# All pair blocks first, all single blocks last, in the expert stage of a two-layer kernel

## The chip, the cores and the metric

The kernel runs on one core of a Trainium2 chip. The metric is the device time in microseconds of one execution. Before the change three runs took 1934.67, 1937.21 and 1942.63 us; the median is 1937.21 us.

The engines are TensorE (PE), VectorE (DVE), ScalarE (ACT), GpSimd (POOL) and SyncE (SP). SP computes nothing here: it issues DMA transfers, in program order, and waits on semaphores between them. POOL issues the transfers that go by an index table.

## The reference, cut to what matters

The whole computation is two layers, each of an attention and a feed-forward part. The change touches only the last part, a mixture of experts over 1600 tokens of width 512, with seven routed experts of which each token takes two, and one shared expert that every token takes:

```python
gate = (xt @ Wr + br) / TEMP
_, ids = jax.lax.top_k(gate + gate_bias, TOPK)         # TOPK = 2 of 7 experts
probs = softmax over the two chosen logits
u = jnp.einsum('nh,ehi->eni', xt, Wup) + bup[:, None, :]
g = jax.nn.silu(jnp.einsum('eni,eij->enj', u, Wgate) + bgate[:, None, :]) * u
eo = jnp.einsum('enj,ejh->enh', g, Wdown) + bdown[:, None, :]
out = jnp.einsum('ne,enh->nh', probs, eo) + shared expert of the same form
```

All matrices are 512 x 512 in fp32, so one expert has three matrices (up, gate, down) of 1 MiB each.

## The kernel before, in words

The kernel works through four stages one after the other; the expert stage (`expert_ffn`) is the last. It runs through 26 **blocks** of tokens, numbered j = 0 to 25. A tile is 128 tokens. Blocks 0 to 5 are the shared expert on two tiles each, block 6 is the shared expert on its thirteenth and last tile. Blocks 7 to 25 are the routed ones: 12 **pairs** (two tiles of one expert) and 7 **singles** (one tile). Which expert a block belongs to is found at run time by the router, whose result lies in a table of slots; how many pairs and singles there are, and at which block number each stands, is fixed in the list `ROUTED` (line 1967), from which `is_pair(j)`, `place_of(j)`, `table_tile(j, i)`, `version_of(j)` and the other small functions follow. In the list of before, a pair and a single alternate as long as there are singles, and five pairs are left over: pairs at blocks 7, 9, 11, 13, 15, 17, 19 and 21 to 25, singles at blocks 8, 10, ..., 20.

A pair and a single are computed in different ways. A pair splits each fp32 operand into a high and a low part in a rounded format and multiplies three times (high x high, low x high, high x low). Its weights land in `ex_raw_weights`, ACT copies them into `ex_weights_high` (line 2264), and DVE subtracts to get `ex_weights_low` (line 2380). The raw buffer of a matrix is free for the next pair as soon as the low part is made. A single multiplies plain fp32 from `raw_s`, a second set of three buffers in memory that held the activations before (the profile calls it `residual`). A buffer of `raw_s` is free only when PE has done the matmuls that read it. There is one such buffer for each matrix.

PE's order (at the end of `expert_ffn`): `gate(j)`, `up(j+1)`, `down(j)`, `turn(j+2)` for each j, where `turn` transposes the gathered rows of a block. Up of a pair is line 2823, up of a single 2819; gate is 2854 and 2848; down is 2877 and 2871; turn is 2797.

SP's order (from line 2229): for j = 7 to 25, it reads the expert of the block and issues three loads, up, gate, down. Ahead of each load of a pair it waits until the low part of the previous pair's matrix is made. Ahead of each load of a single it waits until PE has finished with that matrix in the single before (`single_before(j)`): the up matmuls, the gate matmuls, or all down matmuls.

POOL gathers the rows of block j+3 during block j, makes the low half of a pair's product `g` (line 2766), and adds the finished tiles of the block before into `out` by indirect transfers (line 2735). ACT makes the high parts, the silu and the first output tile, DVE the low parts, the product and the second output tile. A pair's u is kept in `uh` and `ul`, and DVE reads u for the product from PSUM; a single's u lies in `us`, of which there is one buffer, and DVE reads it there.

Of the kernel before, what the change touches and what calls it, by code (L numbers as in the profile page):

```python
# [24 lines left out]
KC = D // 128  # L25
# [1923 lines left out]
NP = (RT - E) // 2  # L1949
NS = RT - 2 * NP  # L1950
# [7 lines left out]

def routed_order():

    order = []
    for k in range(max(NP, NS)):
        order += [("pair", k)] * (k < NP) + [("single", k)] * (k < NS)
    return order


ROUTED = routed_order()


def is_pair(j):  # L1970
    return j < SH_TILES // 2 or (j >= SH and ROUTED[j - SH][0] == "pair")
# [40 lines left out]
def version_of(j):  # L2012

    return 0 if j < SH else pairs_before(j) - pairs_before(SH) + 1
# [17 lines left out]
def expert_ffn(core, w_exp, b_exp, b_down, w_router, b_router, order, tokens, out):  # L2032
# [5 lines left out]
    with ExitStack() as own:  # L2038
# [3 lines left out]
        def sem(name):  # L2042
            return core.sem(tag + name)
# [68 lines left out]
        g_psum, g_silu, g_mul, g_high, g_low = sem("g_psum"), sem("g_silu"), sem("g_mul"), sem("g_high"), sem("g_low")  # L2112
# [4 lines left out]
        def width(j):  # L2117
            return BT * tiles_of(j)

        def new_weights(j):  # L2120
            return SH <= j < BLOCKS and is_pair(j)

        def upb(j, c, n):
            return ps[:, 6 * (j % 2) + c % 2, c // 2 * BN:c // 2 * BN + n]
# [10 lines left out]
        def bias_of(j, m, c):  # L2135
            v = place_of(j) + 1 if j >= SH else 0
            return bsel[:, v, m * KC + c:m * KC + c + 1]
# [37 lines left out]
        with nc.Block() as block:  # L2175
# [77 lines left out]
            def _(act):  # L2253
                def high(v, m):
                    act.wait_ge(w_in[m], (v + 1) * 16)
                    if v:
                        i = pair_before(first_block(v))
                        if m == UP:
                            act.wait_ge(u_psum, (i + 1) * KC)
                        elif m == GATE:  # L2260
                            act.wait_ge(g_psum, (i + 1) * KC)
                        else:
                            act.wait_ge(d_psum, first_tile(i + 1))
                    act.copy(wh[:, m, :], raw[:, m, :]).then_inc(w_high[m], 1)  # L2264
# [27 lines left out]
                def up_high(j):  # L2292
                    n = width(j)
                    act.wait_ge(bias_ready, 1 if j < SH else 2)
                    for c in range(KC):
                        act.wait_ge(u_psum, j * KC + c + 1)
                        dst = uh if is_pair(j) else us
                        act.activation(dst[:, c, :], upb(j, c, n), ACT.Identity, bias=bias_of(j, UP, c)).then_inc(u_high, 1)
                        if c == 1 and new_weights(j):
                            high(version_of(j), GATE)  # L2300
# [38 lines left out]
                block_high(0)  # L2339
                high(0, GATE)  # L2340
                up_high(0)
                high(0, DOWN)
                act.wait_ge(d_exp, 1)
                act.activation(hit[:], hit[:], ACT.Exp).then_inc(r_exp, 1)
                block_high(1)
                for j in range(BLOCKS):
                    gate(j)
                    if j == 0:
                        turn_probs(0)
                    if j + 1 < BLOCKS:  # L2350
                        up_high(j + 1)
                    if j == 0:
                        turn_probs(1)
                    if new_weights(j + 2):
                        high(version_of(j + 2), UP)
                    if j == SH:
                        act.wait_ge(tab_in, 16)
                    first_out(j)
                    if new_weights(j + 1):
                        high(version_of(j + 1), DOWN)  # L2360
                    if j + 2 < BLOCKS:
                        block_high(j + 2)
# [707 lines left out]
```

## Time and profile before

| what | value |
|---|---|
| median of 3 runs | 1937.21 us (1934.67 to 1942.63) |
| profiled execution | 1938.36 us, of which the span of instructions is 1936.2 us |
| granted TensorE clock, mean | 0.981 of full speed |
| routed blocks 7 to 25 with the drain | about 1631 us to the end of the span |

The profiled execution is one run under the hardware profiler. "Busy" counts time in which an engine executes, without its waits. A time in the rows is counted from the span's start. Matmuls overlap, so the difference between two starts says more than one duration. PEclk is the TensorE clock granted, in parts of full speed (2.4 GHz); 0.50 is 1.2 GHz.

### The profile page before, as it was taken

How to read it: one execution, taken by the hardware profiler on the slowest of the kernel's cores; microseconds unless marked ns; L12 is line 12 of the kernel's file. 1: busy time of each engine (PE TensorE's matmuls, PEld its weight loads, DVE VectorE, ACT ScalarE, POOL GpSimd, SP SyncE). 2: the span in 40 equal slices, each digit the busy share in tenths (PEclk: the TensorE clock that was granted, in tenths of full speed). 3: DMA queues.
4: the chain of work that ended last, by engine and by line, in shares of the span. 5: the costliest groups of instructions: out<-in, count | busy, mean ns of one | idle time of the engine just before them, and what ended most of it. 6: DMA issues, size and time to landing. Idle time of an engine off the chain costs nothing. (4 is left out here: it accounts for less than half of the span.)

```text
span 1936.2 us, 30897 instructions
## 1 busy us (share of the span) xinstructions
PE 1788.7 (92%) x11108; PEld 1427.5 (74%) x11122; DVE 1318.7 (68%) x2912; ACT 913.4 (47%) x2005; POOL 600.3 (31%) x582
## 2 busy tenths in 40 slices
PE   8899999999899999999997999899987989999997
PEld 7677887778777887778775544666665878888896
DVE  6777677776687778887777896477676633444564
ACT  3544445433543445434543654555544324555563
POOL 5333122331633122321211131232231454343353
PEclk9999999999999999999998999899999989999999
DMA  5022211210121222222204111000005267787773
GB/s 213 17 89 86 65 42 69 89 61 33 67 79 37 95 80 67 76 97 81 81 17 206 36 40 39 25 1 1 1 22 171 59 190 224 241 282 265 238 236 77
DMA packets 49672, 188.52 MB, mean 97 GB/s; under 512 B 7388, under 2 KB 11612, under 8 KB 38260
## 3 DMA queue, kind: packets, MB, share of 16 engines
q1 hardware_dynamic: 39396, 166.86, 23.9%
q0 software_dynamic: 9840, 19.70, 5.3%
q8 instruction: 91, 1.49, 0.3%
q14 instruction: 57, 0.47, 0.1%
q10 hardware_dynamic: 288, 0.00, 0.0%
HBM read 158.29 MB, written 28.24 MB: 96 GB/s over the span
## 5 line engine op out<-in xcount | busy, mean ns | idle before, releaser
L442 POOL TENSOR_TENSOR la_q_roped<-la_q_roped 128x400 f32<-128x400 f32 x128 | 134.7, 1074 | 657.2 <-DVE la_q_roped L976 657.2
L869 ACT ACTIVATE la_probs<-banks,la_minus_max 100x361 f32<-100x361 f32 x256 | 144.8, 566 | 179.5 <-DVE la_minus_max L1087 179.5
L976 DVE TENSOR_TENSOR la_q_roped<-banks,la_rope_q 128x400 f32<-128x400 f32 x384 | 198.0, 567 | 34.9 <-PE banks L557 26.1
L611 PEld LDWEIGHTS banks<-identity,la_probs 100*121 100x121 f32 x768 | 111.2, 184 | 78.6 <-DVE la_probs L1094 54.1
L1094 DVE TENSOR_SCALAR la_probs<-la_probs,la_rsum 100x361 f32<-100x361 f32 x256 | 154.8, 605 | 9.1
L650 PE MATMUL banks<-la_ctx_parts,la_wout_high 128*128 128x416 f32 (+3 forms) x512 | 158.6, 361 | 2.0 <-DVE residual L1028 1.7
L611 PE MATMUL banks<-identity,la_probs 100*121 100x100 f32 x768 | 127.5, 274 | 31.2 <-DVE la_probs L1094 18.8
L1087 DVE TENSOR_REDUCE la_minus_max<-banks 100x1 f32<-100x361 f32 x256 | 134.8, 527 | 28.0 <-PE banks L602 26.0
L2380 DVE TENSOR_TENSOR ex_weights_low<-ex_raw_weights,ex_weights_high 128x2048 fp32r<-128x2048 f32 x39 | 89.4, 2292 | 93.5 <-ACT ex_weights_high L2264 93.5
L622 PE MATMUL banks<-la_probs_t,la_kv_rows 121*128 121x200 f32 x768 | 152.3, 334 | 0.0
L887 ACT COPY la_probs_t<-banks 121x300 f32<-121x300 f32 x256 | 104.8, 409 | 60.3 <-PE banks L611 60.0
L622 PEld LDWEIGHTS banks<-la_probs_t,la_kv_rows 121*128 121x128 f32 x768 | 132.0, 190 | 0.3
L797 ACT CAST la_q_high<-banks 128x400 fp32r<-128x400 f32 x64 | 31.6, 495 | 179.5 <-PE banks L539 179.5
L1107 DVE TENSOR_TENSOR la_ctx_parts<-banks,la_ctx_parts 128x200 fp32r<-128x200 f32 (+2 forms) x144 | 48.0, 342 | 94.8 <-ACT la_ctx_parts L879 94.5
L602 PE MATMUL banks<-la_kv_t_high,la_qk_high 128*100 128x362 f32 x256 | 101.6, 397 | 2.9 <-ACT la_probs L869 2.7
L1300 PE MATMUL banks<-qf_sign_weights,qf_x_quant_t 128*128 128x512 bf16 (+1 forms) x403 | 95.8, 390 | 6.4 <-DVE qf_hidden L1435 2.9
L574 PE MATMUL banks<-la_q_roped,la_weights 128*64 128x400 f32 x512 | 96.6, 508 | 4.9 <-POOL la_q_roped L442 4.9
L650 PEld LDWEIGHTS banks<-la_ctx_parts,la_wout_high 128*128 128x128 f32 x512 | 95.5, 189 | 6.3 <-DVE residual L1028 3.3
L2766 POOL TENSOR_TENSOR ex_g_low<-ex_g,ex_g_high 128x256 fp32r<-128x256 f32 x72 | 56.7, 831 | 134.0 <-ACT ex_g_high L2312 133.8
L539 PE MATMUL banks<-la_xn_t_high,la_wq_high 128*128 128x400 f32 x256 | 95.9, 375 | 0.8 <-DVE la_xn_t_low L951 0.8
L2735 POOL DMA_INDIRECT out<-ex_block_out,ex_slots x31 | 57.0, 1840 | 118.8 <-ACT ex_block_out L2324 110.0
L1659 POOL TENSOR_TENSOR ca_probs<-ca_probs,ca_rsums 100x400 f32<-100x400 f32 x64 | 54.7, 855 | 123.2 <-DVE ca_rsums L1882 122.9
(380 smaller groups left out, 5055.1 us busy)
## 6 DMA issues: line engine op xcount, KB each, us to landing
ex_raw_weights<-w_exp SPq DMA_DIRECT2D x39, 1024.0 KB
la_weights<-w_pack SPq DMA_DIRECT2D x15, 1856.0 KB, 7.7
residual<-w_exp SPq DMA_DIRECT2D x24, 1024.0 KB, 7.5
la_kv_turned<-w_ffn SPq DMA_DIRECT2D x30, 384.0 KB
la_rope_k<-w_ffn SPq DMA_DIRECT2D x30, 384.0 KB, 3.4
qf_sign_weights<-ffn_signs SPq DMA_DIRECT2D x3, 2048.0 KB, 7.9
ffn_signs<-la_ffn_signs SPq DMA_DIRECT2D x30, 192.0 KB, 2.0
out<-ex_block_out POOLq DMA_DIRECT2D x13, 256.0 KB
```

The lines of the kernel that those rows point to most:

```text
L442: pool.tensor_tensor(roped[:, h, 0, c, :], roped[:, h, 0, c, :], roped[:, h, 1, 1 - c, :], ALU.add).then_inc(b_add, 1)
L539: mm = pe.matmul(ps[:, unit_bank(n, u), 0:NT], a[:, k, wc], b[:, k, xs], start=(k == 0 and j == 0), stop=(k == KC - 1 and j == 2))
L574: mm = pe.matmul(ps[h * R:(h + 1) * R, C_BANKS[run], 0:NT], w["r"][:, j, h, :], roped[:, h, v, c, :], start=(j == 0), stop=(j == len(STEPS ...
L602: mm = pe.matmul(ps[0:S, j % 2, 0:LE], a[:, h, qs], c[:, b, :], start=(k == 0), stop=(k == 2))
L611: mm = pe.transpose(ps[0:LC, T_BANK, c * S:(c + 1) * S], prob[:, j % 4, c * LC:(c + 1) * LC], core.ident[0:S, 0:S])
L622: mm = pe.matmul(ps[:, V_BANK, 0:2 * S], kv[:, b, c, :], probt[:, b % 2, c, :, :].rearrange("p h s -> p (h s)"), start=(c == 0), stop=(c = ...
L650: mm = pe.matmul(ps[:, out_bank(n, run, k), 0:count], a[:, h, kc], c[:, h, :], start=(h == 0 and j == 0), stop=(h == 1 and j == 2))
L869: act.activation(prob[:, s % 4, 0:L], ps[0:S, s % 2, 0:L], ACT.Exp, bias=nmax[:, s % 4:s % 4 + 1], accum_out=sums[:, s % 4:s % 4 + 1]).the ...
L887: act.copy(probt[:, b % 2, :, j % 2, :], ps[0:LC, T_BANK, 0:LCN * S].rearrange("p (c s) -> p c s", c=LCN)).then_inc(t_out, 1)
L976: dve.tensor_tensor(roped[:, h, v, c, :].rearrange("p (b s) -> p b s", b=GB), ps[:, B_BANKS[k % 2], 0:NT].rearrange("p (b s) -> p b s", b=GB),
L1087: dve.tensor_reduce(nmax[:, s % 4:s % 4 + 1], ps[0:S, s % 2, 0:L], AX.X, ALU.max, negate=True).then_inc(s_max, 1)
L1094: dve.tensor_scalar(prob[:, j % 4, 0:L], prob[:, j % 4, 0:L], rsum[:, j % 4:j % 4 + 1], None, ALU.mult).then_inc(s_norm, 1)
```

## The change

The list of routed blocks is put in another order: the 12 pairs stand first, at blocks 7 to 18, and the 7 singles last, at blocks 19 to 25. Every engine's program is generated from this list, so loads, gathers, copies, matmuls and scatters all move with it; their number stays the same. Since singles now follow each other, and `us` is a single buffer, ACT gets a wait in `up_high`: before it writes u of a single that follows a single, all products of the block before must be done.

```diff
 def routed_order():
-    order = []
-    for k in range(max(NP, NS)):
-        order += [("pair", k)] * (k < NP) + [("single", k)] * (k < NS)
-    return order
+    return [("pair", k) for k in range(NP)] + [("single", k) for k in range(NS)]
...
                 def up_high(j):
                     n = width(j)
                     act.wait_ge(bias_ready, 1 if j < SH else 2)
+                    if not is_pair(j) and not is_pair(j - 1):
+                        act.wait_ge(g_mul, j * KC)
                     for c in range(KC):
                         act.wait_ge(u_psum, j * KC + c + 1)
```

Here NP = 12, NS = 7, SH = 7 (the number of shared blocks) and KC = 4 (chunks of 128 in a width of 512).

## Rows read from the trace of the kernel before

**Rows 1.** The head of the page: busy time of each engine.

```profile
PE 1788.7 (92%) x11108; PEld 1427.5 (74%) x11122; DVE 1318.7 (68%) x2912; ACT 913.4 (47%) x2005; POOL 600.3 (31%) x582
```

**Rows 2.** Windows: length, busy PE, PEld, DVE, ACT, POOL, clock, DMA share, GB/s.

```profile
1779.69:1809.45 29.76, 29.37 (x205) 25.98 (x205) 13.35 (x17) 15.90 (x28) 11.08 (x10) 1.00 0.80 265
1839.26:1857.38 18.12, 18.12 (x128) 16.89 (x129) 12.54 (x14) 12.11 (x18) 8.64 (x8) 1.00 0.77 258
1857.38:1875.23 17.85, 17.85 (x131) 16.84 (x130) 12.26 (x14) 11.82 (x18) 11.01 (x9) 1.00 0.73 223
```

**Rows 3.** Waits of PE, 1600 to 1905: total us, times, longest.

```profile
PE banks L2854 <- issue: 2.7, 7, 0.4
```

**Rows 4.** Chain of waits, around a single, then a pair round: start, us.

```profile
1808.62 0.44 PE banks L2797 x4
1809.06 0.39 issue
...
1815.44 1.78 PE banks L2819 x16
...
1819.28 5.48 PE banks L2877 x24
...
1825.63 3.57 PE banks L2848 x32
...
1834.95 3.43 PE banks L2871 x8
...
1857.62 5.76 PE banks L2854 x48
1863.38 5.75 PE banks L2823 x48
1869.13 5.47 PE banks L2877 x24
```

**Rows 5.** Timeline of DVE, the low part of turned rows: start, us.

```profile
1860.99 1.22 DVE L2389 TENSOR_TENSOR ex_block_t_low<-banks,ex_block_t_high 128x1024 fp32r<-128x1024 f32 x1
```

**Rows 6.** Timeline of SP's queue: a single's down load, then two of a pair.

```profile
1808.79 0.33 SPq L2245 DMA_DIRECT2D residual<-w_exp  x1
1809.88 0.85 SPq L2245 DMA_DIRECT2D ex_raw_weights<-w_exp  x2
```

**Rows 7.** Timeline: two loads issued together, and ACT's wait for the second.

```profile
1843.71 1.47 SPq L2245 DMA_DIRECT2D ex_raw_weights<-w_exp  x2
...
1852.51 1.92 ACT L2264 CAST ex_weights_high<-ex_raw_weights 128x2048 fp32r<-128x2048 f32 x1 [0.72 <-DMA ex_raw_weights<-w_exp]
...
1879.09 1.43 SPq L2245 DMA_DIRECT2D ex_raw_weights<-w_exp  x2
...
1888.31 1.91 ACT L2264 CAST ex_weights_high<-ex_raw_weights 128x2048 fp32r<-128x2048 f32 x1 [0.81 <-DMA ex_raw_weights<-w_exp]
```

**Rows 8.** Landing after issue: routed loads (line 2245); three together (2227).

```profile
DMA to landing us min/median/max: 5.3/7.6/8.2
...
DMA to landing us min/median/max: 7.0/7.0/7.0
```

**Rows 9.** Windows at two gaps of PE, and PE's timeline at the second.

```profile
1550.50:1554.50 4.00, 0.00 (x0) 0.00 (x0) 0.75 (x1) 0.00 (x0) 0.00 (x0) 0.75 0.54 149
1554.50:1559.30 4.80, 4.78 (x23) 4.78 (x24) 1.23 (x1) 1.23 (x2) 0.00 (x0) 0.50 0.97 386
1594.60:1600.20 5.60, 5.54 (x13) 4.37 (x14) 0.00 (x0) 0.69 (x1) 2.06 (x3) 0.50 0.28 47
...
1594.66 0.79 PE L2877 MATMUL banks<-ex_weights_high,ex_g_high 128*128 128x512 f32 x1 [3.38 <-POOL ex_g_low L2766]
```

**Rows 10.** Timeline of DVE: last product of a single.

```profile
1829.64 0.29 DVE L2413 TENSOR_TENSOR residual<-residual,ex_silu_gate 128x128 f32<-128x128 f32 x1 [0.60 <-issue]
```

**Rows 11.** Timeline of POOL: the scatter of a single, and the last scatter.

```profile
1809.62 1.62 POOL L2735 DMA_INDIRECT out<-ex_block_out,ex_slots  x1 [9.38 <-ACT ex_block_out L2324]
...
1925.06 1.55 POOL L2735 DMA_INDIRECT out<-ex_block_out,ex_slots  x1 [1.01 <-DVE ex_block_out L2432]
```

## The prediction

> **What bounds the kernel now.** I read the engine totals first: TensorE (PE) is busy for 92% of the span, no other engine over 68% [rows 1]. The change touches only the routed blocks of the last stage, so all else is read there. The windows show what one round of the present order (one pair block and one single block) costs: 29.76 us with PE busy for 29.37 of it, and one round of the pair blocks that already stand together at the end: 17.85 us with PE busy for all of it, the first of two alike [rows 2]. Over the routed stretch PE waits 2.7 us in all, 0.4 us at a time, and for no load [rows 3]. So this stretch is bound by matmuls, and the order of blocks can gain little on PE: the arithmetic is the same. The question is what the loads do when the blocks that PE finishes fastest, each with 3 MiB of weights, stand together.
>
> The chain of waits gives the phases (differences of starts) [rows 4]. Pair: gate 5.76, up 5.75, down 5.47, and the rest of the 17.85 us for turn, 0.87. Single: up 3.84 (1815.44 to 1819.28), gate 3.57, down 3.43, turn 0.44 and 0.39 until the turned-out bank is free (0.83 together), in all 11.67 us. PE's order is gate(j), up(j+1), down(j), turn(j+2).
>
> **The pair run (blocks 7 to 18).** What is moved: 12 pair blocks stand together, with their 36 weight loads on SP's queue, 24 gathers and 24 scatter-adds on POOL's, and the high and low copies of weights on ACT and DVE. The last blocks of the old order are just that, and there the weight copies, gathers and scatters all fit in 17.85 us with no idle PE: ACT is busy 11.8 us of it, DVE 12.3, POOL 11.0 [rows 2]. The smallest cover I see is the low half of the next block's turned rows: DVE ends it at 1862.2 (1860.99+1.22) and PE's up starts at 1863.38 [rows 4, 5], about 1.2 us of slack. I cost the run at 17.85 per block, nothing extra; if the cover were gone, it would be some 1 us for each of ten blocks. The entry (single 6, pair 7, pair 8) is the same sequence as single 20, pair 21, pair 22 of before, whose first round took 18.12 [rows 2].
>
> **The single run (blocks 19 to 25).** The singles work from one raw buffer per matrix, each refilled only after its last use, and SP issues in program order: UP(j), GATE(j), DOWN(j), then UP(j+1). DOWN(j) has to wait until down(j-1) is over. Call that moment T. UP(j+1) stands behind it on SP, though up(j) was over 3.4 us earlier. In the old order that does no harm: the next thing behind a single's DOWN is a pair's load into another buffer, and the next single is a whole pair block away: down ended at 1808.62, DOWN was issued at 1808.79, and the load behind it at 1809.88 [rows 4, 6]. In the new order that load is UP(j+1), and PE wants it after turn (0.83) and gate(j) (3.57), at T+4.4.
>
> When does it arrive? Issue is at T+0.17 and T+1.26 by these rows. Three times before, SP issued two 1 MiB loads 1.1 us apart and ACT then waited for the second; in the first and the last of them the issue is at 1843.71 and 1879.09, ACT's copy starts at 1852.51 and 1888.31 [rows 7]. That is 8.80 and 9.22 us after the first issue, with POOL's gather of two tiles going on beside it. In the single run one scatter and one gather fall on the same place, so I take 9.0, between the two: UP(j+1) is there at T+9.2, and PE idles **4.8 us**. From both sides: a lone 1 MiB load landed in 5.3 us at best and 8.2 at worst [rows 8]; three issued at once landed 7.0 after their issue, nothing beside them [rows 8]. The second can't be earlier than about 7.4 after the first issue by that (stall 3.2), and with the worst lone row plus the 1.1 us and some more contention it is 10.3 (stall 6.1).
>
> The Trainium skill, page "DMA: Bandwidth & Descriptors", section "Anatomy of one DMA — SWDGE (gpsimd) path", fits a transfer as about 2.0 us fixed plus its bytes over 436 GB/s; for 2 MiB that makes an estimate of 6.8 us instead of the 9.0 read above, a stall of 2.6. The rows with other traffic beside decide for me; the fit belongs with the second rival.
>
> How often? UP(19), GATE(19), DOWN(19) go into buffers idle since block 6 and are issued behind pair 18's loads, one pair block early: hidden. UP(20) waits only for up(19), since DOWN(19) was issued long before; PE wants it after down(18), turn and gate(19), 5.47+0.83+3.57 = 9.9 us later, against 5.3 to 8.2 for a lone load [rows 4, 8]: hidden. UP(21), 22, 23, 24, 25: stalled. **Five stalls.** GATE(j+1), issued when gate(j) ends, has over 13 us; DOWN(j), the first of the two, lands before up(j+1) ends. DOWN(25), behind T of the last round, lands some 5.3 us later, when the last gate's result is ready anyhow (0.83+3.57+about 1): nothing.
>
> **The clock.** PE's granted clock is full (2.4 GHz) in these rounds [rows 2]. Earlier in the same stage it fell twice: after 4.0 us without PE work (1550.5 to 1554.5) the next 4.8 us ran at 0.50 (1.2 GHz), and after a gap of 3.38 us (to 1594.66) the next 5.6 us did [rows 9]. Gaps of 4.8 us are longer than both. Half of 4.8 and of 5.6 us is 2.4 and 2.8 lost. The slow stretch ended 8.8 us after the first gap began (1550.5 to 1559.3) and 8.9 us after the second (1591.3 to 1600.2), so with PE back only after 4.8 us there would remain 4.0 to 4.1 us at half speed, 2.0 lost. I take **2.3 us** per stall; bounds 0 (no fall) and 3.3 (a slow stretch half as long again).
>
> The Trainium skill speaks against this change: "TensorE: Matmul & The Clock Gate", section "HAM oscillation — how this bites in real kernels", describes a loop in which each wait for a load drops the clock again, so that each next piece starts cold. This trace agrees in its two gaps; that it would happen five times in a row no row of it shows.
>
> **The added wait.** ACT's up_high of a single after a single waits for the last product of the block before, since both use one u buffer. Behind it on ACT are that block's silu, its output copy, and PE's third up chunk. The last product of a single's gate ended at 1829.93 (1829.64+0.29) [rows 10], 0.73 us after gate's end (1825.63+3.57), and the first up chunk isn't finished before 3.84/4 = 0.96 us after that end: nothing. In the single run up comes after a stall besides. Uncovered it is under 1 us for each of six, so up to 6 in all, and below nothing there is no gain in a wait.
>
> **What is saved.** The mixed round costs 29.76 against 17.85+11.67 = 29.52: 0.24 us for each of the six whole rounds, 1.4 us [rows 2, 4]. At the end, a single drains faster than a pair: the last pair's second tile goes out in a second scatter at 1925.06, waiting for DVE, with 1936.2 as the end, and its down needs a low half that POOL makes [rows 11]. A single has no low half and one scatter, which starts 1.0 us after its down (1808.62 to 1809.62) [rows 4, 11]. I take 1.1 us. Together **-2.5 us** (bounds 0 and -5).
>
> **Sum.** 5 x (4.8 + 2.3) = 35.5, less 2.5 = +33 us on the profiled execution's 1938.36 (span 1936.2 and 2.2 around it): 1971. That execution stands 1.2 above the median 1937.21 of the runs shown, so the forecast is **1970 us**. Its own range is 1962 to 1977.
>
> **Rivals.**
> A. The stalls come, the clock holds. For it: the two falls are single gaps, and rows of repeated ones don't exist here; against it: both are shorter than 4.8 us. 5 x 4.8 - 2.5 = +21.5: 1959. Chance 0.12.
> B. The loads land sooner, because in the single run far less goes over DMA in a round (3 MiB and two tiles in over 16 us, against 6 MiB and six tiles in 29.76). Then the stall is 3.2 and the clock falls sometimes: 5 x 3.2 to 5 x 4.2, less 2.5: +13 to +18, 1951 to 1956. Chance 0.12. The skill's DMA fit named above would give 5 x 2.6 - 2.5 = +10.5, 1948, the low end of this.
> C. More goes wrong in the same direction: landing at T+10.4 and a loss of 3.3, or the pair run's 1.2 us of cover is gone. 5 x 9.3 - 2.5 = +44, 1981, or 1970 + 10. Chance 0.13.
> D. Not slower: UP(j+1) is there when PE wants it, and only the 2.5 us are left, 1935. It is decided at SP's queue: the second load would have to land within 4.2 us of the first issue, where even a lone first one took 5.3. It would be so if SP had passed the wait on down(j-1) already, which the code excludes. For it speaks only that before no single's load was waited for. Chance 0.05.
> The forecast has 0.58.
>
> **Numbers.** About 0.5% (10 us) is what a measurement of this kernel can tell from no change. Slower by more: forecast, A, C and nearly all of B, 0.93. Within 0.5%: D and the low end of B, 0.06. Faster: 0.01. The range is 1951 to 1982: it takes in A, B from its row-based low end, and C.
>
> **What would show it.** Right: the timeline of PE's up phase of blocks 21 to 25 has five gaps before it of 4 to 6 us, ended by the DMA of the single buffer; the clock row has 0.50 right after each; SP issues DOWN(j) 0.2 us after down(j-1) ends and UP(j+1) 1.1 us later; pair rounds are 17.85 us with no gap and lie from about 1631 to 1843; single rounds are near 18.8 us instead of 11.7. The last round's down shows no such gap. Wrong: single rounds near 11.7 us (D), rounds near 16.5 us at full clock (A), gaps before gate or down as well, or pair rounds over 18 us (C). A gap before block 20's up would be a miscount of the stalls, some 7 us each.

## The result, and the profile after

The new kernel takes 1973.46 us (median of 4 runs, 1972.84 to 1974.51) against 1938.31 us of the old one beside it; the ratio is 1.0175, 95% interval 1.0160 to 1.0189. It is slower by 35 us. Forecast was 1970 us, 33 us more.

The head of the page after: PE is still busy for 92% of the span, but the last two of the 40 slices of the clock row, which were 9 before, are 8. The last row below is the clock row of the old kernel.

```profile
span 1970.5 us, 30911 instructions
PE 1804.3 (92%) x11122; PEld 1442.3 (73%) x11122; DVE 1319.2 (67%) x2912; ACT 914.0 (46%) x2005; POOL 613.2 (31%) x582
...
PEclk9999999999999999999999998999999999999988
...
PEclk9999999999999999999998999899999989999999
```

The windows of the new kernel, in the columns of [rows 2]: two rounds of pairs, then four rounds of singles, and last the first gap of PE in the single run.

```profile
1650.98:1668.83 17.85, 17.85 (x131) 16.84 (x130) 12.27 (x13) 11.82 (x18) 10.58 (x8) 1.00 0.76 228
1668.83:1686.68 17.85, 17.85 (x131) 16.84 (x130) 12.26 (x13) 11.81 (x18) 10.92 (x9) 1.00 0.80 237
...
1874.11:1891.80 17.69, 13.12 (x78) 10.79 (x77) 1.17 (x4) 4.11 (x10) 2.57 (x2) 0.90 0.60 207
1891.80:1911.60 19.80, 14.43 (x79) 12.10 (x77) 1.17 (x4) 4.10 (x10) 2.58 (x2) 0.83 0.53 187
1911.60:1929.29 17.69, 13.12 (x79) 10.79 (x77) 1.17 (x4) 4.10 (x10) 1.56 (x1) 0.90 0.56 193
1929.29:1949.28 19.99, 14.33 (x77) 11.69 (x74) 1.17 (x4) 4.10 (x10) 1.56 (x1) 0.83 0.50 171
...
1860.10:1863.90 3.80, 0.00 (x0) 0.00 (x0) 0.29 (x1) 0.37 (x1) 0.00 (x0) 0.91 1.02 303
```

The pair rounds are what they were in [rows 2], 17.85 us with no idle PE. A single round takes 17.7 to 20.0 us (18.8 on average) where its phases add up to 11.67 [rows 4]. Over a whole round the DMA engines are *less* busy than before (0.50 to 0.60, against 0.80 in a mixed round), though they are fully busy (1.02) within the first gap, when the loads have at last been issued. That speaks for a late issue and not for a lack of rate over the round; the experiments test it.

PE's waits from 1600 on, as in [rows 3], now have one large line. Line 2818 is the up of a single; the profile names no releaser ("issue").

```profile
PE banks L2818 <- issue: 22.5, 5, 5.3
PE banks L2847 <- issue: 2.4, 5, 0.8
PE banks L2847 <- DMA residual<-w_exp: 0.7, 1, 0.7
PE banks L2870 <- DMA residual<-w_exp: 0.7, 1, 0.7
```

The chain of waits shows where the five lie, in the form of [rows 4]: after gate (2847), before up (2818). Two of them:

```profile
1870.67 3.44 PE banks L2870 x8
1874.11 0.44 PE banks L2796 x4
1874.55 0.39 issue
1874.93 3.81 PE banks L2847 x32
1878.74 4.18 issue
1882.93 5.44 PE banks L2818 x32
1888.37 3.44 PE banks L2870 x8
...
1892.62 3.81 PE banks L2847 x32
1896.43 4.98 issue
1901.41 6.75 PE banks L2818 x32
```

The gaps are 3.89, 4.18, 4.98, 4.18 and 5.26 us, and up after them runs for 6.70, 5.44, 6.75, 5.44 and 6.64 us, where it takes 3.57 behind a single's gate without a gap. SP's queue at the first of the two, and the landing of the second load in it, as in [rows 6, 8]: down's load is issued 0.17 us after down(j-1) ended at 1874.11, up's 1.1 us later. Up's load lands 7.5 us after its own issue, at 1882.9, which is when up starts. For the five stalls that landing took 7.5, 7.5, 7.9, 7.5 and 8.5 us.

```profile
1874.28 1.43 SPq L2242 DMA_DIRECT2D residual<-w_exp  x2
...
DMA to landing us min/median/max: 7.5/7.5/7.5
```

To compare traces without what lies ahead of the changed part, I use the stretch from the start of block 6's gate to the end of the span: 319.0 us before (1617.17 to 1936.2), 351.7 after (1618.8 to 1970.5), **+32.7 us**. The remaining 1.6 us of the two spans' difference was there before block 6, in blocks that are the same; the executions of the old kernel alone differ by 8 us. Where I speak of "the stretch" below, it is this one, in the profiled execution of each run.

### The profile page after: what moved, and what is told of

Read it like the earlier page. It is cut to its first block and busy times, and to the rows that moved or that the text cites. A ratio compares the mean times of both kernels' runs of the same rounds, so it can differ in the third digit from the quotient of the medians.

```text
span 1970.5 us, 30911 instructions
## 1 busy us (share of the span) xinstructions
PE 1804.3 (92%) x11122; PEld 1442.3 (73%) x11122; DVE 1319.2 (67%) x2912; ACT 914.0 (46%) x2005; POOL 613.2 (31%) x582
## 5 line engine op out<-in xcount | busy, mean ns | idle before, releaser
L2765 POOL TENSOR_TENSOR ex_g_low<-ex_g,ex_g_high 128x256 fp32r<-128x256 f32 x72 | 60.8, 950 | 143.7 <-ACT ex_g_high L2311 143.4
```

## The experiments

The theory: up(j+1) stands in SP's program order behind a wait on down(j-1) that it doesn't need itself, lands late, and the gap makes the clock fall. Rivals were the rate of the DMA engines, the added wait on ACT, and slow reads in place of a slow clock. Each run is compared with runs of the old kernel on the same chip, whose median was between 1937.5 and 1940.4 us.

### Up's load ahead of down's

```diff
+                loads = [(j, m) for j in range(SH, BLOCKS) for m in range(MATS)]
+                for j in range(SH + NP + 1, BLOCKS - 1):
+                    at = loads.index((j, DOWN))
+                    loads[at:at + 2] = [(j + 1, UP), (j, DOWN)]
...
```

> New order of blocks; in the single run SP issues up(j+1) ahead of down(j), and nothing else is changed. Theory (queue order: the up load stands behind a wait on down(j-1) that it doesn't need): up(j+1) is issued 3.4 us earlier and lands near the end of gate(j); down(j) lands some 8 us after down(j-1), just when it is wanted. Gaps of 0 to 1 us, no fall of the clock, 1935 to 1942 us. Rival 1 (3 MiB per single round of 11.7 us are more than the DMA engines carry): the gaps move ahead of down or gate and stay about 4 us, 1958 to 1975. Rival 2 (the wait that the change adds on ACT): 1973, as after.

Measured: 1940.29 us, ratio 0.9992 (0.9978 to 1.0006); the stretch takes 316.3 us. One swap in the order of issue, in each of five rounds, gives the whole loss back. The same bytes move in rounds of 11.8 us, so the rate of the DMA engines was not the limit. The chain now goes through the gate loads, which just fail to be early (0.6 us at most): line 2854 (gate of a single) follows a load of 7.7 us.

```profile
1853.60 3.82 PE banks L2854 x32
...
1857.58 7.72 DMA residual<-w_exp
1865.30 0.08 issue
1865.37 3.82 PE banks L2854 x32
```

### Two sets of buffers

```diff
+                            i = single_before(j) if j == SH + NP else j - 2
+                            if j == SH + NP + 1:
+                                sp.wait_ge(w_low[m], NP + 1)
...
+                            dst, arrived = single_mats(j)[:, m, :], single_in(j, m)[0]
```

> New order of blocks; the singles of the last run use two sets of weight buffers in turn, their own and the one that the pairs have left free, so that each load waits for the block two before. SP's order is unchanged. Theory: no gap is left, 1934 to 1938 us, i.e. 35 us come back, and the 2.5 us that the order itself saves can be seen. Rival 1 (rate of the DMA engines): with buffers to spare the rate still holds, rounds above 13 us, over 1945. Rival 2 (wait on ACT): 1973.

Measured: 1937.02 us, ratio 0.9982 (0.9970 to 0.9994); stretch 315.3 us. SP's order is the old one, but its waits are on the block two before, so the load behind them is early. The profile shows no wait of PE that a load ended, and none over 0.8 us, and rounds take 11.64 us by the starts of down:

```profile
1864.58 3.44 PE banks L2883 x8
...
1868.84 3.81 PE banks L2860 x32
1872.65 3.57 PE banks L2831 x32
1876.22 3.44 PE banks L2883 x8
```

### Four singles last

```diff
-    return [("pair", k) for k in range(NP)] + [("single", k) for k in range(NS)]
+    mixed = [x for k in range(3) for x in (("pair", k), ("single", k))]
+    return mixed + [("pair", k) for k in range(3, NP)] + [("single", k) for k in range(3, NS)]
```

> Order of blocks: three rounds of pair and single, then nine pairs, then four singles. Theory (the first two singles of a run find their loads ready, each later one stalls): two stalls of 7 us, less 2: 1950 us, two gaps ahead of up in the trace. Rival (a run of singles stalls from its second block on, or the cost is that of the long pair run): 1957, or no change against the run of seven, 1973.

Measured: 1954.98 us, ratio 1.0071 (1.0050 to 1.0093), which is 5 us more than expected; stretch 330.2 us, 11.2 more than before, where 12 was expected. PE waits ahead of up twice, 4.28 and 5.67 us, and the up after each takes 5.18 and 5.92 us. In a last run of four two stall, in one of seven five: the count holds.

### The gap filled with matmuls

```diff
+                        if j >= SH + NP + 2:
+                            pe.wait_ge(g_mul, (j - 2) * KC + 3)
+                            for _ in range(18):
+                                pe.matmul(upb(j, 0, n), core.ident[:], core.ident[:], start=True, stop=True)
                         pe.wait_ge(s_in[UP], 16 * (singles_before(j) + 1))
```

> New order of blocks; PE runs 18 fp32 matmuls on the identity (0.22 us each, 4.0 us) ahead of the up of blocks 21 to 25, into the bank that up then overwrites. They fill the gap with work that nobody needs. Theory (gap plus a fall of the clock that follows from it): the gap stays as long as the load takes, but the clock stays at 1.00 and up runs in 3.57 us in place of 5.3 to 6.6: 12 us less, 1961 us. Rival (up is slow because its operands come late or DMA traffic slows the reads, not by the clock): up stays at 5.3 to 6.6 us, 1973.

Measured: 1965.49 us, ratio 1.0121 (1.0099 to 1.0142), some 10 us below the new kernel by the ratios; stretch 343.5. The windows over two rounds show the clock at 1.00 (so do those over the other three):

```profile
1858.00:1876.00 18.00, 15.88 (x115) 13.44 (x115) 1.17 (x4) 4.83 (x12) 2.64 (x3) 1.00 0.60 205
1876.00:1893.00 17.00, 15.60 (x114) 13.24 (x114) 1.17 (x4) 4.16 (x11) 2.62 (x3) 1.00 0.64 217
```

and the chain names what the profile of the new kernel called "issue": SP issues down's load (line 2242), then reads the expert (2228), then up's load runs, and PE's up (2822) starts as it lands and takes 3.84 us.

```profile
1871.51 3.45 PE banks L2874 x8
1875.11 0.33 SPq L2242
...
1875.49 0.27 SPq L2228
...
1876.20 8.36 DMA residual<-w_exp
1884.61 3.84 PE banks L2822 x32
```

The slow up was the clock. 1961 was too low: of the 12 us expected, 8.2 came on the stretch. Four of the five loads of up landed 8.4 to 8.9 us after their issue here, against 7.5 to 8.5 in the new kernel. From the end of down(j-1) to the start of up it was 48.9 us over the five rounds, against 46.0, so some 3 us went there. Why they landed later no run shows.

### A quarter of down's bytes

```diff
+                        if m == DOWN and j > SH + NP:
+                            sp.dma_start(dst[:, 0:D], w_exp[bass.ds(e, 1), m, :, 0:D].rearrange("e p d -> p (e d)")).then_inc(arrived, 16)
+                            continue
```

> New order of blocks; in blocks 20 to 25 the down load moves only the first 512 of 2048 columns of its matrix (256 KiB in place of 1 MiB), so the rest of the down weights is left out. The wait on down(j-1) and SP's order stay. Theory (up(j+1) is late by its place in the queue, and how late depends on the bytes ahead of it): up lands some 2.3 us sooner, five gaps of 2.0 to 2.5 us in place of 4.5; such gaps let the clock fall at most now and then; 1938 - 2.5 + 11 = 1947 us, up to 1955 if the clock falls each time. Rival (the landing is latency, whatever is ahead): gaps of 4.5 us, 1970.

Measured: 1950.65 us, ratio 1.0055 (1.0039 to 1.0070); stretch 335.1 us. Four gaps are 2.0 to 2.5 us, as the theory said, and one is 4.6, which it did not; 13.4 in all (the first, of 2.04, isn't in the rows below; up took 5.44 after it), against 22.5. So with 768 KiB less ahead of it up's load lands sooner, mostly by some 2 us; the other 7 us or so from the end of down(j-1) to its landing stay. Why one gap stayed long is open. What I hadn't expected is that the clock fell after three of the five gaps, short ones among them:

```profile
1873.69 2.22 issue
1875.90 3.81 PE banks L2821 x32
...
1887.79 4.62 issue
1892.40 5.42 PE banks L2821 x32
...
1905.89 2.05 issue
1907.94 3.81 PE banks L2821 x32
...
1919.82 2.51 issue
1922.33 5.44 PE banks L2821 x32
```

### Two buffers for u, without the added wait

```diff
-                    if not is_pair(j) and not is_pair(j - 1):
-                        act.wait_ge(g_mul, j * KC)
...
-                        dst = uh if is_pair(j) else us
+                        dst = uh if is_pair(j) else us_of(j)
```

> New order of blocks; the singles' u lies in two buffers in turn, so the added wait of ACT on the products of the block before is not needed and is gone. Weights and SP's order as in the new kernel. Theory (the wait is hidden): 1973 us, within 2 us of the new kernel, five gaps of 3.9 to 5.3 us as there. Rival (the wait holds ACT up, and through it PE's third chunk of up): rounds of singles get shorter by up to 1 us each, 1967.

Measured: 1976.65 us, ratio 1.0185 (1.0168 to 1.0201), which overlaps the new kernel's interval. The five gaps ahead of up are there as well, 4.2 to 6.0 us and 25.4 in all, somewhat more than the 22.5 of the new kernel. Taking the wait away gives nothing.

### Twos in turn

```diff
...
+    order = []
+    for k in range(0, NP, 2):
+        order += [("pair", k), ("pair", k + 1)] + [("single", i) for i in (k, k + 1) if i < NS]
+    return order
```

> Order of blocks: two pairs, two singles, in turn, and pairs for the rest (the last single alone). One set of buffers as in the new kernel. Theory (in a run of n singles only n-2 stall, since the first two find the buffers free long before): no stall at all, although singles follow each other; 0 to 2 us below before. Rival (a single behind a single stalls): three gaps, 1955 to 1960.

Measured: 1975.70 us, ratio 1.0178 (1.0163 to 1.0193); stretch 353.2 us. Both expectations were wrong: three gaps, but of 10 us each, and ahead of *gate* of the second single. The timelines of SP and ACT at one of the three show why. SP issues the second single's down load at 1749.1, when the first single's down is over, and only then, at 1750.19, the next pair's up load. ACT, in order, stands for 11.39 us at the high copy of that very matrix, and the output copy (2326) that frees PE's bank for the next gate is behind it:

```profile
1742.08 7.34 SPq L2245 DMA_DIRECT2D residual<-w_exp  x2
1750.19 1.37 SPq L2245 DMA_DIRECT2D ex_raw_weights<-w_exp  x3
...
1757.28 1.90 ACT L2264 CAST ex_weights_high<-ex_raw_weights 128x2048 fp32r<-128x2048 f32 x1 [11.39 <-DMA ex_raw_weights<-w_exp]
1759.08 0.68 ACT L2326 ACTIVATE ex_block_out<-banks,ex_slots 128x512 f32<-128x512 f32 x1
...
1749.79 10.07 issue
1759.86 6.05 PE banks L2850 x32
```

So the same wait on SP, with another load behind it, costs more. My rule (n-2 of a run stall) was borne out only for runs at the very end (four and seven singles), with no pair behind.

### Twos, with the pair's up load earlier

```diff
...
+                    if not is_pair(j - 1) and not is_pair(j) and is_pair(j + 1):
+                        loads.remove((j + 1, UP))
+                        loads.insert(loads.index((j, GATE)), (j + 1, UP))
...
```

> Order of blocks as in the run with twos (two pairs, two singles, in turn); SP issues the up load of the pair that follows two singles ahead of the second single's gate and down loads. Theory formed on the trace of the twos (the three gaps of 10 us come from that load standing on SP behind the wait on the first single's down, while ACT, in order, waits for it ahead of the output copy that frees PE's bank): the three gaps go, 35 us come back, 1936 to 1942 us. Rival (a single behind a single is slow in itself, by its own loads or banks): three gaps of 5 us or more stay, over 1955.

Measured: 1951.93 us, ratio 1.0072 (1.0053 to 1.0090); stretch 330.3 us. Neither number was hit. 23 of the 34 us come back on the stretch, and the gaps of 10 us are down to 0.8 or 0.9 us each ahead of the single's gate. Three smaller gaps (8.5 us in all) now stand a block later, ahead of the pair's gate, where ACT waits 3.58 us for a further weight load, at 1755.97, again with an output copy behind it. Behind two of these gaps (3.07 and 3.01 us) the clock falls and the pair's gate takes 7.46 and 7.48 us in place of 5.76; behind the third (2.43) it stays at 1.00 and the gate takes 6.17. The two rows are from ACT's timeline at the third:

```profile
1755.97 1.90 ACT L2272 CAST ex_weights_high<-ex_raw_weights 128x2048 fp32r<-128x2048 f32 x1 [3.58 <-DMA ex_raw_weights<-w_exp]
1757.77 0.68 ACT L2334 ACTIVATE ex_block_out<-banks,ex_slots 128x512 f32<-128x512 f32 x1
```

### Both pairs of buffers

The edit joins that of the two sets with that of the two u buffers.

> New order of blocks, with two sets of weight buffers for the last singles and two buffers for u, so that neither loads nor ACT's added wait can hold a single up. Theory: as with two sets alone, 3 us below before (0.1 to 0.2%), since ACT's wait costs nothing; the stretch from block 6's gate to the end takes 315 us in place of 319.0. Rival (ACT's wait costs something once the loads no longer hide it): 1 to 3 us less than with two sets alone, 313 us or less for that stretch.

Measured: 1936.40 us, ratio 0.9981 (0.9967 to 0.9994); stretch 315.2 us, against 315.3 with two sets alone. ACT's wait costs nothing here either. With 0.2% it is the best version beside that with two sets, and both are faster than the old kernel by about as much as can be told.

## Why the prediction was right

**The pair run** was costed at 17.85 us a block and nothing extra. It took that, and from block 6's gate to the single run PE shows no wait. (The rows bear out the block time; the cover of 1.2 us was not tested.)

**The place and the number of the stalls** were right: five, ahead of the up of blocks 21 to 25. The two experiments on SP (order, buffers) show the cause, since each leaves the bytes and the order of blocks alone and brings the time back.

**The stall** was put at 4.8 us (24.0 in all); measured 22.5, or 4.5 each. Up was to be there 9.2 us after down(j-1)'s end and was there after 8.9, 8.8, 9.6, 8.8 and 9.9, on average 9.2. The two waits of [rows 7], which had a gather of two tiles beside them, were good measures for it. What was too short is the other side: PE wanted up 4.6 us after that end and not 4.4, because the gate of a single behind the short wait for the bank takes 3.81 us and not 3.57, and in the first round 5.0, because that gate waited for its own load besides.

**The clock** was put at 2.3 us a stall (11.5). Up took 30.97 us in the five rounds in place of 5 x 3.57 = 17.85, so 13.1 us more; 0.27 of each is the start after any gap (3.84 with the clock at 1.00, in the run with the filled gap), which leaves 11.8. Rival A (the clock holds) is out. The sum is right, but in part by luck. The working had the slow stretch end about 8.8 us after the gap began; it ended 8.4 to 11.2 us after, and the loss was 1.6 us behind two gaps and 2.8 to 2.9 behind three. The 2.3 lies between the two kinds. The Trainium skill, page "TensorE: Matmul & The Clock Gate", section "HAM oscillation — how this bites in real kernels", describes a loop in which the wait for each load drops the clock again. The new kernel's trace agrees: it fell anew in each of five rounds.

**What is saved** was put at 2.5 us. The runs with the stalls removed show it alone: 316.3, 315.3 and 315.2 us against 319.0, so 2.7 to 3.8 less. Counted up from the 315.3 of the two sets, the gaps (22.5), the slower up (13.1) and 0.5 more for short waits make 351.4, against 351.7 measured. So the saving was nearer 3.7, a little more than forecast. How it divides between the rounds (1.4 by the forecast) and the end (1.1) no run shows.

**The added wait** was put at nothing: shown twice.

**Rival B** had the stall at 3.2 us, because far less goes over DMA in a single round. Less did go (a busy share of 0.50 to 0.60), but the second load landed no sooner for it, and the smallest gap was 3.89 us. The Trainium skill, page "DMA: Bandwidth & Descriptors", section "Anatomy of one DMA — SWDGE (gpsimd) path", has a fit by which the two loads would take an estimated 6.8 us. It is given for transfers that GpSimd issues, and these come from SP. The trace shows 8.6 us from the first issue at 1874.28 to 1882.9, and up to 9.6 in the other rounds.

**Missed, but small:** gate of block 20 waited 0.7 us for its load. The prediction gave every gate load over 13 us of cover, which counts a stall in between; ahead of block 20 there is none yet, and the cover is only the 7.4 us of up, down and turn, against a landing 8.1 us after the end of the gate before. Down of block 25 waited 0.7 us as well, where I had called it nothing and had counted a turn (0.83 us) that the last round doesn't have.

A weak point that luck hid: I counted stalls by asking only when each *single's* load is free to go. The twos showed that every load behind the waiting one has to be followed, through ACT too. In the new order there is no pair behind the run, so the count came out.

## What to carry to other kernels

SP's queue here issues loads in program order with waits between them, and so a load goes out no sooner than the last wait ahead of it ends, whether it needs that wait or not. Before blocks of a kind are put together, write down for each load which wait stands before it in the queue, when that wait ends, and when the load is wanted; if the wait belongs to a later use than the load's own, swap them or give the buffer a twin. Follow the load to the end, through the engines that wait for it in order. And add the clock: behind the five gaps of 3.9 to 5.3 us it cost another 1.6 to 2.9 us each. Behind the three gaps of 10 us in the run with twos it was no more: the gate took 5.45, 6.05 and 6.25 us in place of 3.84.

## What I had not expected of the hardware

The stretch at 0.50 was 3.4 or 6.8 us long in the clock's records of the new kernel, in turn with the gaps (3.89: 6.8; 4.18: 3.4; 4.98: 6.8; 4.18: 3.4; 5.26: 6.8), and up ran 5.4 or 6.7 us by it. The windows over two ups show it, in the columns of [rows 2]; the first of them began at full clock, which fell only 0.8 us after PE had resumed.

```profile
1882.93:1888.37 5.44, 5.44 (x33) 5.44 (x34) 0.00 (x0) 1.10 (x3) 0.00 (x0) 0.69 0.53 218
1901.41:1908.17 6.76, 6.75 (x33) 6.76 (x34) 0.00 (x0) 1.10 (x3) 0.00 (x0) 0.54 0.33 136
```

Gaps of 2.04 and 2.51 us were followed by a fall and gaps of 2.05 and 2.22 us were not, in one execution of one kernel. So the length of the gap alone doesn't decide it, at 2 us.
